# An expert loop whose results ScalarE brings out, a ring of eight for the scatter indices, and a later place for the pads

## What is computed

```python
x = x + attn(_layernorm(x), ...)       # gated delta rule, 8 heads of 128, a scan over 2048 tokens
x = x + ffn(_layernorm(x), ...)        # mixture of experts

# ffn: 8 experts, the two best per token
logits = flat_x @ W_router + b_router
top_vals, top_idx = jax.lax.top_k(logits, 2)
router_weights = softmax(logits of the two, -inf elsewhere)
for e in range(8):
    h = relu(flat_x @ W1[e] + b1[e])   # 128 -> 512
    y = h @ W2[e] + b2[e]              # 512 -> 128
    final_output += y * router_weights[:, e, None]   # 0 for tokens that did not choose e
```

## Time and profile before

| | us |
|---|---|
| median of 3 runs | 1470.88 (1468.65 to 1473.63) |
| the profiled execution | 1456.88 |
| its span | 1454.8 |
| busy in the span: TensorE, VectorE, ScalarE, GpSimd | 1207.4, 1158.9, 823.5, 728.8 |
| attention part, to the last group's second half (x2.1) | 0 to 1237.3 |
| last group's router and scatter, table of tiles | 1237.3 to 1260.0 |
| expert loop, first turn to last result | 1261.2 to 1422.1 |
| last scatter, closing sums, output | 1422.1 to 1454.8 |

### The profile page before, as it was taken

One profiled execution on the slowest core, in us unless ns is written; L12 is line 12 of the kernel. 1 busy time (PEld: TensorE's weight loads), 2 busy tenths in 40 slices (PEclk: granted clock), 3 DMA queues, 4 the chain that ended last, 5 costly groups with the idle time before them and its releaser, 6 DMA issues.

```text
span 1454.8 us, 33709 instructions
## 1 busy us (share of the span) xinstructions
PE 1207.4 (83%) x11978; PEld 985.3 (68%) x11978; DVE 1158.9 (80%) x2567; ACT 823.5 (57%) x2497; POOL 728.8 (50%) x601
## 2 busy tenths in 40 slices
PE   0356999999898989898989898989999896389980
PEld 0234868787787878786878686868777775267760
DVE  6878888888888788979788888888888853677774
ACT  1243666566656656575657666666565654255552
POOL 3143645546373737373737465555646341154544
PEclk9986989899999989999989998999999898699996
DMA  6031221213131303131222221221212152322214
GB/s 199 4 91 30 68 66 37 74 37 76 36 82 36 86 27 91 31 92 30 81 42 69 43 68 45 66 74 38 74 37 76 35 147 69 98 61 65 65 46 173
DMA packets 163174, 97.07 MB, mean 67 GB/s; under 512 B 115623, under 2 KB 148269, under 8 KB 161988
## 3 DMA queue, kind: packets, MB, share of 16 engines
q1 hardware_dynamic: 124932, 82.25, 20.8%
q10 hardware_dynamic: 33536, 4.20, 2.0%
q0 software_dynamic: 4544, 8.47, 1.8%
HBM read 73.31 MB, written 24.61 MB: 67 GB/s over the span
## 4 chain that ended last, share of the span: by engine, by line
PE 57%; DVE 15%; ACT 10%; issue 7%; DMA 6%; POOL 2%; SPq 1%; POOLq 1%; ACTq 0%; DVEq 0%
PE kx L1539 7%; PE ob L1640 4%; PE rc L1597 4%; PE rc L1606 4%; PE ob L1625 4%; PE ob L1626 4%; PE rc L1588 3%; PE rc L1589 3%; PE rc L1590 3%; DMA rows_out<-rhs,e_dst 3%; PE rc L1614 2%; DVE blkT L1061 2%; PE pj L1551 2%; ACT area L775 2%; DVE Y_sb L1057 2%
## 5 line engine op out<-in xcount | busy, mean ns | idle before, releaser
L639 POOL TENSOR_TENSOR kq<-tapA,area 128x256 f32<-128x256 f32 x256 | 198.7, 785 | 290.0 <-DVE area L1147 289.0
L1057 DVE TENSOR_TENSOR Y_sb<-blkT,blkN 128x4 f32<-128x4 f32 (+18 forms) x304 | 163.5, 538 | 10.4
L766 ACT ACTIVATE area<-pj,taps 128x256 f32<-128x256 f32 x256 | 120.7, 471 | 86.4 <-PE pj L1553 83.6
L1144 DVE SCALAR_TENSOR_TENSOR tapA<-pj,taps,tapA 128x256 f32<-128x256 f32 x256 | 122.2, 477 | 58.6 <-ACT tapA L766 57.1
L622 POOL TENSOR_TENSOR kq<-kq,area 128x1024 f32<-128x1024 f32 x64 | 152.4, 2382 | 0.0
L611 POOL DMA_INDIRECT rows_in<-rowbuf,dest x64 | 66.2, 1035 | 171.5 <-DVE dest L1133 146.2
L1061 DVE TENSOR_REDUCE blkT<-Y_sb 128x2 f32<-128x4 f32 (+18 forms) x304 | 142.2, 468 | 4.7
L1539 PE MATMUL kx<-kq 128*128 128x128 f32 x1024 | 138.4, 285 | 9.1 <-ACT GTs L849 5.1
L1539 PEld LDWEIGHTS kx<-kq 128*128 128x128 f32 x1024 | 126.1, 197 | 17.5 <-issue 11.1
L668 POOL DMA_INDIRECT rows_out<-rhs,e_dst x78 | 79.7, 1022 | 88.9 <-DVE e_dst L1326 47.9
L1147 DVE SCALAR_TENSOR_TENSOR area<-pj,taps,area 128x256 f32<-128x256 f32 x256 | 121.4, 474 | 0.0
(11 more groups left out here) (306 smaller groups left out, 3631.0 us busy)
## 6 DMA issues: line engine op xcount, KB each, us to landing
area<-scr_alpha SPq DMA_DIRECT2D x32, 512.0 KB, 4.3
area<-scr_acum SPq DMA_DIRECT2D x32, 512.0 KB, 4.2
blkN<-scr_n SPq DMA_DIRECT2D x32, 256.0 KB, 3.9
area<-rows_in SPq DMA_DIRECT2D x39, 130.0 KB, 2.3
scr_n<-area SPq DMA_DIRECT2D x128, 32.0 KB, 1.6
area<-rows_out SPq DMA_DIRECT2D x4, 1024.0 KB, 8.1
rows_in<-rows_in SPq DMA_DIRECT2D x8, 260.0 KB, 3.6
kq<-in_x SPq DMA_DIRECT2D x4, 512.0 KB, 6.0
```

Source lines behind the costliest of these rows:

```text
L639: nc.gpsimd.tensor_tensor(dst[:, n % H, :], tapA[:, n % RING, :], tapB[:, n % RING, :], ALU.add).then_inc(conv_done, 1)
L766: ins = nc.scalar.activation(dst[:, n % RING, :], pj[n % 2][:, k:k + GT], ACT.Copy, scale=taps[:, t, k:k + 1])
L1057: ins = nc.vector.tensor_tensor(p4, bc(blkT[:, r0:, j:].rearrange("p r (o m) -> p r o m", o=1), [128, nr, w, wd]), bc(blkN[:, j:j + w, j:] ...
L1144: nc.vector.scalar_tensor_tensor(out=tapA[:, n % RING, :], in0=pj[n % 2][:, 0:GT], scalar=taps[:, order[n], 0:1], in1=tapA[:, n % RING, :] ...
```

## The change

Four parts, all in or around the expert stage:

1. `e_dst` has eight places, and `low(t)` waits for the scatter of tile t - 8.
2. `results` goes from VectorE to ScalarE, an activation with Copy, with the wait for tile t - 4's scatter ahead of it, since `y_rows` keeps its four places.
3. `pads` stands at step `ti` of the last pass instead of step `sc`.
4. The closing sums are all VectorE's: after each piece's eight instructions comes its addition of 128 x 1024; GpSimd has none, and `c_last` goes.

```diff
+    DRING = 8
...
-                    if step == "sc" and isinstance(g, int) and g == NG - 1:
+                    if step == "ti" and isinstance(g, int) and g == NG - 1:
                         pads()
...
-        e_dst = sb("e_dst", [128, 4, 2], U32)
+        e_dst = sb("e_dst", [128, DRING, 2], U32)
...
-            for q in range(PIECES - 1):
-                pool.wait_ge(c_first, q + 1)
-                pool.wait_ge(c_second, q + 1)
-                rows_q = slice(PC * q, PC * q + PC)
-                nc.gpsimd.tensor_tensor(x_sb[:, rows_q, :], x_sb[:, rows_q, :], y_parts[q][:, :, 0, :], ALU.add).then_inc(c_done, 1)
...
+            def results(t):
+                act.wait_ge(e_down, t + 1)
+                if t >= 4:
+                    act.wait_ge(e_out[t % 4], 32 * (t // 4))
+                nc.scalar.activation(y_rows[:, t % 4], rc[t % 2][:, 0:TT].rearrange("p (b d) -> p b d", d=D), ACT.Copy,
+                                     scale=1.0 / WSCALE).then_inc(e_y, 1)
...
                     hidden(t + 1)
+                results(t)
...
-                if t >= 4:
-                    dve.wait_ge(e_out[t % 4], 32 * (t // 4))
-                nc.vector.tensor_tensor(e_dst[:, t % 4, :], e_rows[:, t % 4, :, D].bitcast(I32), tab_far[:, t, :],
+                if t >= DRING:
+                    dve.wait_ge(e_out[t % 4], 32 * (t // 4 - 1))
+                nc.vector.tensor_tensor(e_dst[:, t % DRING, :], e_rows[:, t % 4, :, D].bitcast(I32), tab_far[:, t, :],
                                         ALU.max).then_inc(e_dest, 1)
...
-            def results(t):
-                dve.wait_ge(e_down, t + 1)
-                nc.vector.tensor_scalar(y_rows[:, t % 4], rc[t % 2][:, 0:TT].rearrange("p (b d) -> p b d", d=D), 1.0 / WSCALE, None,
-                                        ALU.mult).then_inc(e_y, 1)
...
             for q in range(PIECES):
+                rows_q = slice(PC * q, PC * q + PC)
                 dve.wait_ge(y_in[q], 16)
...
                 ins.then_inc(c_second, 1)
+                dve.wait_ge(c_second, q + 1)
+                dve.wait_ge(c_first, q + 1)
+                nc.vector.tensor_tensor(x_sb[:, rows_q, :], x_sb[:, rows_q, :], y_parts[q][:, :, 0, :], ALU.add).then_inc(c_done, 1)
```

More of the change, by code:

```diff
@@ L220, in preln_delta_moe_kernel @@
         e_in, e_out, y_in = sems("e_in0 e_in1 e_in2 e_in3"), sems("e_out0 e_out1 e_out2 e_out3"), sems("y_in0 y_in1 y_in2 y_in3")
-        (e_turn, e_xhi, e_xlo, e_up0, e_up1, e_relu0, e_relu1, e_hi, e_lo, e_down, e_y, e_dest, c_first, c_second, c_done, c_last, f_out) = sems(
-            "e_turn e_xhi e_xlo e_up0 e_up1 e_relu0 e_relu1 e_hi e_lo e_down e_y e_dest c_first c_second c_done c_last f_out")
+        (e_turn, e_xhi, e_xlo, e_up0, e_up1, e_relu0, e_relu1, e_hi, e_lo, e_down, e_y, e_dest, c_first, c_second, c_done, f_out) = sems(
+            "e_turn e_xhi e_xlo e_up0 e_up1 e_relu0 e_relu1 e_hi e_lo e_down e_y e_dest c_first c_second c_done f_out")
         block = ctx.enter_context(nc.Block())
@@ L550, in _ @@
             for q in range(PIECES):
[L551 to L554, removed]
+                sp.wait_ge(c_done, q + 1)
                 sp.dma_start(yt[:, q * PC:q * PC + PC, :], x_sb[:, q * PC:q * PC + PC, :]).then_inc(f_out, 16)
@@ L668, in _ @@
                     nc.gpsimd.indirect_dma_start(
-                        rows_out, bass.IndirectOffsetOnAxis(ap=e_dst[:, t % 4, b:b + 1], axis=0), y_rows[:, t % 4, b, :], None,
+                        rows_out, bass.IndirectOffsetOnAxis(ap=e_dst[:, t % DRING, b:b + 1], axis=0), y_rows[:, t % 4, b, :], None,
                         bounds_check=2 * TOKENS - 1, oob_is_err=False).then_inc(e_out[t % 4], 16)
-            for q in range(PIECES - 1):
-                pool.wait_ge(c_first, q + 1)
-                pool.wait_ge(c_second, q + 1)
-                rows_q = slice(PC * q, PC * q + PC)
-                nc.gpsimd.tensor_tensor(x_sb[:, rows_q, :], x_sb[:, rows_q, :], y_parts[q][:, :, 0, :], ALU.add).then_inc(c_done, 1)
         @block.scalar
@@ L1359, in _ @@
                     hidden(t + 1)
-                results(t)
                 if t == 1:
```

## The result

The median of 4 runs is 1434.31 us (1428.69 to 1451.83), beside 1469.77 us for the kernel before (4 runs, 1467.62 to 1473.63): a ratio of 0.9743, 95% interval 0.9698 to 0.9788. The forecast was 1440.5 with a range from 1435 to 1452. The profiled execution took 1428.69 us, its span 1426.8, with a mean granted clock of 0.92.

The account below looks back on a forecast made before the run. The prediction took VectorE's waits for earlier scatters, a ring of two tiles, to hold the loop at 4.04 us per tile. Terms of 21.1, 6.7 and 2.6 us, together 30.4, off the 1470.88 median gave 1440.5 us, range 1435 to 1452.

Parts of the forecast that it names:

- The loop, -21.1: Expert loop: with the scatter wait opened, TensorE bounds at 3.40 us per tile, 135.0 us instead of 156.07.
- The bias table's period: Early loop period where VectorE makes the other tiles' bias table: stays, at most, at 5.45 us.
- The pads, -6.7: Before the loop: residual load goes ahead of the pads, so the second sum starts at 1230.55 instead of 1237.29.
- The closing sums, -2.6: Kernel end: VectorE additions of 1.22 us end the sums at 1445.8 instead of 1448.06, last output issued alone.
- The step from the profile to the median: Whole kernel: the profile-to-median difference of 14 us stays, so 30.4 us come off the 1470.88 median.
- the prediction's 0.3%: Whole kernel: about 4.4 us is what a measurement can tell from no change.
- 4 us low: Low end of the range, 1435: reached if the bias table costs less and the runs fall 4 us low.
- B: Loop: TensorE still held now and then, 3.72 us per tile, giving back 10.9 us: 1451.4; chance 0.12.
- C: Closing sums: VectorE's additions keep their 3.25 us, giving 1448.2; chance 0.05.
- D: Before the loop: pads hidden anyway, or late landings give the 6.7 us back: 1447.2; chance 0.07.
- E: Loop does not move, scatter wait returning on ScalarE or through GpSimd; only 9.3 us remain: 1461.6; chance 0.04.
- F: Loop slower through TensorE's clock: at 0.75 it takes 180 us, giving 1485.5; chance 0.03.

Follow-up runs that it names:

- the pair: Changed kernel with SyncE holding the third closing output until the fourth is ready: 1452.12 us, ratio 0.9837, beside the changed kernel's 1454.55 on the same chip.
- the ring alone: Kernel before with only the eight-place e_dst, results staying on VectorE: 1470.73 us (0.9972) on the second chip, 1438.15 us (0.9823) on the third.
- the kernel with two edits more: Changed kernel with eight closing pieces and the late bias table in two parts: 1456.14 us (0.9879) on the second chip, 1428.25 us (0.9759) on the third.

## Why the prediction was right, and where not

**The loop, -21.1: right.** From the turning of tile 2 to the last result, 1264.56 to 1399.53, are 134.97 us; 135.0 was forecast. TensorE's 3.40 us per tile held 32 times in a row. The bias table's period was 5.06 instead of "at most" 5.45 us, and the way from the last turning to the last result 9.61 instead of 9.23. VectorE's and ScalarE's loads were forecast at 2.7 and 2.8 us per tile; by the second stretch above they are 15.80 and 16.25 of 20 us, 2.7 and 2.8. That the ring opens the loop was right; the move, which the sum doesn't need since VectorE's 3.08 us lay below TensorE's 3.40 already, is worth nothing that shows (139.9 against 139.7).

**The pads, -6.7: right.** The second sum came 4.45 us behind the first instead of 11.14, released by TensorE, which was named as late next. GpSimd's scatter waits for VectorE's destinations as before, not for the pads:

```profile
1250.29 1.03 POOL L609 DMA_INDIRECT rows_in<-rowbuf,dest  x1 [6.04 <-DVE dest L1132]
```

**The closing sums, -2.6: this term was mis-sized, it measured -5.7.** Its working held up to the end of the sums: additions of 1.22 us, sums 13.8 us long where 14.05 was forecast (1409.33 to 1423.13). The step that failed is the last one, "the last output goes out alone, not 0.4 us behind another". It took what lies behind the sums as unchanged but for the distance between two issues. Before, the span ends 6.7 us after the last addition, because that addition is GpSimd's and its drain takes 6.5 us from there; changed, it ends 3.7 us after it, with the one output. Of these 3.0 us, 1.8 are also the price of the pair (the run with it has 5.5 us), and 1.2 are what the drain takes beyond that. In the prediction's own terms the sum should have been 33.5 us, which would have made the forecast 1437.4, inside the range and above the measured 1434.31 still.

The rule of the Trainium skill, page "SBUF — State Buffer", section "SBUF: two separate sides", that VectorE's addition and GpSimd's exclude each other, agrees with the trace both ways: 1.22 us without GpSimd's, 3.24 when they are put back.

**The step from the profile to the median.** The difference was taken from the median, since "nothing in the trace tells where these lie" of the 14 us between profile and median. The stretches suggest where: in the attention part, which took from 1225.3 to 1244.8 us over profiles in which its code is the same. That part of a run doesn't cancel in a median of four, whose runs lie 23 us apart; twelve runs of the kernel before beside each other lie as far apart (1454.73 to 1477.33), so the prediction's 0.3% for what a measurement can tell was too small for so few runs. The profiles show this between profiled executions only; where the other runs spend their time isn't recorded. The low end of 5.5 us below the forecast allowed only "4 us low" for it, and nothing for a closing term too small; 3.1 us of term and about as much of spread put the median 0.7 us outside. On the two other chips with the short loop the changed kernel had 1436.33 and 1432.18 us, the first inside the range, the second outside.

**Rivals.** B (3.72 us per tile) did not come: no period after the fourth differs from 3.40. C fell with the additions of 1.22 us, D with x2.1 at 1235.88, E with TensorE's 20.00 of 20. F did not come as it was put: 1.00 was granted in the loop's stretches, on chip 4 too (1276 to 1430 us). But its thought, that TensorE's pace sets the time once the ring is open, is what the second, fourth and fifth chip show: TensorE late at a granted clock of 1.00 was no rival of the prediction. Where it acts the loop gives nothing that can be told, the ratio is 0.9822 or 0.9882 instead of 0.9743 to 0.9789, and pads and closing sums bring their 12.4 us all the same.

## What to carry to other kernels

A wait for a buffer four tiles back can be the whole difference between an engine's own 3.40 us and a period of 4.04; look for the smallest buffer in the ring (here 128 x 4 x 2 indices) and enlarge that before moving work between engines. At the end of a kernel, look at what ends last there: here it was GpSimd's drain, 6.5 us behind its last addition, so that work taken off GpSimd at the end is worth more than its own length; and price the last output by what the queue still has to carry when it is issued, not by the distance of the issues. And before a variant that fails is believed, run the full change beside it on the same chip: here the ring alone read as worthless on one chip and as worth over 20 us on another. And where rows say that an engine waited for nothing, look at when the semaphore went up, since TensorE's ends are modelled.

## What was not expected of the hardware

- On three of six placements (the second, fourth and fifth chip) opened loops took 155 to 163 us instead of 138 to 140, with the same files: 159.3 against 138.4 for the kernel with two edits more, 159.4 against 139.9 for the ring alone. The granted clock is 1.00 in both. On the fourth chip VectorE stands seven times for 17.6 us in all ahead of one instruction without a releaser shown, and ScalarE's and TensorE's idle times grow with it (TensorE's from 10.3 to 20.6 us ahead of L1690). What ends VectorE's long waits is TensorE's semaphore, up to 3.8 us after the end that its row shows. The kernel before hardly differs there in time (1472.18, 1478.82 and 1468.79 against 1467.62 and 1468.99). Why TensorE is late there is open.
- The attention part, 1226 us in the first profile, took from 1225.3 to 1244.8 us over the profiles, 19.5 us apart, on code that is the same.
- GpSimd's closing drain ends 6.45 to 6.47 us after its last instruction in all 20 profiles, whether that is an addition or a scatter. The span therefore ends 2.0 us after the last transferred byte when GpSimd added last, and 0.8 us when VectorE did.
